# Spacing the indirect DMAs of a routed expert layer by the expert blocks, with TensorE's attention slots put in another order

## The reference

```python
x = x + tanh(g_xattn) * attention(layernorm(x), ctx, ctx)   # 16 heads of 16, 77 keys per batch, float32
x = x + tanh(g_ffn) * moe(layernorm(x))

def moe(x):                        # 4096 rows, 8 experts, W1 (8, 256, 512), W2 (8, 512, 256)
    probs = softmax(x @ Wg)
    top_w, top_i = top_k(probs, 2); top_w = top_w / (sum(top_w) + 1e-8)
    h = square(relu(x @ W1[e])); y = h @ W2[e]        # for the two chosen experts e of a row
    return sum over the two choices of top_w * y
```

## Time and profile before

| | |
|---|---|
| Median of 3 runs | 614.36 us (608.73 to 615.72) |
| The profiled execution | 608.3 us, its span 606.5 us |
| PE busy | 530.1 us (87% of the span) |
| PEld, DVE, ACT, POOL busy | 482.5, 365.5, 277.5, 240.8 us |
| Mean granted clock of TensorE | 0.953 |
| Chain that ended last, by engine | PE 68%, DVE 14%, issue 8%, "another core or an unknown queue" 5% |
| Gathers (L701) | 64, 0.95 us each on POOL |
| Row stores (L692) | 64, 1.02 us each on POOL |

### The profile page before, as it was taken

How to read it: one execution, slowest core, us unless ns; L and a number is a source line. 1 busy time by engine, 2 the same in 40 slices (tenths; PEclk the granted TensorE clock), 3 DMA queues, 4 the chain that set the end, 5 groups by cost and what they waited for, 6 DMA issues and landing times.

```text
span 606.5 us, 13192 instructions
## 1 busy us (share of the span) xinstructions
PE 530.1 (87%) x4125; PEld 482.5 (80%) x4125; DVE 365.5 (60%) x934; ACT 277.5 (46%) x564; POOL 240.8 (40%) x346
## 2 busy tenths in 40 slices
PE   5789999889999999988988699999939997979780
PEld 3688999879898888977777689999839996969670
DVE  5665576585766777854675854454416774736452
ACT  3455455544555453634543345555425553535330
POOL 5154446756677455637126300000343543040422
PEclk9799999999999998978999989999979998989986
DMA  7102222342433531536326463222334775553423
GB/s 252 37 2 89 88 79 65 120 132 84 136 106 96 175 105 36 166 130 202 112 69 194 135 207 110 81 75 77 103 95 145 225 217 166 154 157 107 138 89 120
DMA packets 63873, 73.93 MB, mean 122 GB/s; under 512 B 8128, under 2 KB 56512, under 8 KB 63808
## 3 DMA queue, kind: packets, MB, share of 16 engines
q1 hardware_dynamic: 56560, 55.45, 29.2%
q0 software_dynamic: 6272, 16.79, 8.7%
q10 hardware_dynamic: 976, 0.84, 0.5%
HBM read 42.78 MB, written 32.37 MB: 124 GB/s over the span
## 4 chain that ended last, share of the span: by engine, by line
PE 68%; DVE 14%; issue 8%; another core or an unknown queue 5%; ACT 2%; POOL 1%; DMA 0%; POOLq 0%; DVEq 0%; ACTq 0%
PE pair L931 38%; PE pair L1116 10%; PE pair L1017 5%; PE pair L968 4%; DVE top L1357 3%; PE pair L1118 2%; PE pair L999 2%; PE pair L1177 1%; PE pair L1058 1%; DVE st L1398 1%; PE pair L1038 1%; DVE hsq L1310 1%; DVE attn L1370 1%; DVE xgTlo L1314 1%
## 5 line engine op out<-in xcount | busy, mean ns | idle before, releaser
L701 POOL DMA_INDIRECT ys<-y_scratch,list_at x64 | 60.8, 950 | 192.5 <-DMA y_scratch<-y_sb 133.7
L931 PE MATMUL pair<-w2hi,hThi 128*128 x284 | 86.9, 306 | 9.5 <-issue 5.2
L1300 DVE TENSOR_TENSOR hTlo<-pair,hThi 128x512 fp32r<-128x512 f32 x71 | 49.0, 691 | 66.7 <-ACT hThi L792 47.4
L1310 DVE TENSOR_TENSOR hsq<-pair,hrelu 128x512 f32<-128x512 f32 x71 | 49.0, 690 | 58.8 <-ACT hrelu L798 45.6
L931 PE MATMUL pair<-w1hi,xgThi 128*128 x142 | 64.1, 451 | 23.3 <-DVE xgTlo L1314 23.3
L931 PE MATMUL pair<-w2lo,hThi 128*128 x284 | 81.8, 288 | 0.0
L931 PE MATMUL pair<-w2hi,hTlo 128*128 x284 | 80.7, 284 | 0.0
L1116 PE MATMUL pair<-long,probT 128*128 128x136 f32 x512 | 77.9, 298 | 1.9 <-issue 1.9
L798 ACT ACTIVATE hrelu<-pair 128x512 f32<-128x512 f32 x71 | 42.5, 598 | 72.8 <-PE pair L931 60.3
L692 POOL DMA_INDIRECT xe_scratch<-stage,list_at x64 | 65.5, 1024 | 25.1 <-issue 12.8
L1116 PEld LDWEIGHTS pair<-long,probT 128*128 128x128 f32 x512 | 68.4, 201 | 3.5 <-issue 2.1
(11 more groups left out here) (180 smaller groups left out, 1278.1 us busy)
## 6 DMA issues: line engine op xcount, KB each, us to landing
xg<-xe_scratch SPq DMA_DIRECT2D x71, 128.0 KB
y_scratch<-y_sb SPq DMA_DIRECT2D x71, 128.0 KB
raw<-in_L_ffn_W SPq DMA_DIRECT2D x16, 512.0 KB
xs<-in_x SPq DMA_DIRECT2D x16, 256.0 KB, 3.8
x_scratch<-xs SPq DMA_DIRECT2D x16, 256.0 KB, 2.2
xn_scratch<-xn SPq DMA_DIRECT2D x16, 256.0 KB
stage<-xn_scratch SPq DMA_DIRECT2D x32, 128.0 KB
x1s<-x_scratch SPq DMA_DIRECT2D x32, 128.0 KB, 3.3
```

Source lines behind the costliest of these rows:

```text
L701: pool.indirect_dma_start(ys[t % YB][:, k, :].bitcast(I32), None, y_dram[:, :], bass.IndirectOffsetOnAxis(ap=list_at[:, k, t:t + 1], axis= ...
L931: mm = pe.matmul(dst, l(k), r(k), start=(k == 0 and i == 0), stop=(k == n - 1 and i == 2))
L1300: dve.tensor_tensor(hTlo[j % 2][:, :, :].rearrange("p c n -> p (c n)"), bank[2 + j % 2][:, :], hThi[j % 2][:, :, :].rearrange("p c n -> p ...
L1310: dve.tensor_tensor(hsq[i % 2][:, :], bank[i % 2][:, :], hrelu[:, :], ALU.mult).then_inc(v_hsq, 1)
```

## The change

Row stores: one a slot up to slot 66, two from there (64 as before). From slot 65 on, the first store of a tile waits for the hThi copy of its slot's block j (`a_hT` at j+1) and the second for the hrelu copy of the same call (`a_relu` at j+3). Gathers: `plan_gathers` gives each of the 64 a half-block of its own, with the same kind of waits; each choice has its own semaphore, and VectorE's sum waits for the two one after the other. The sums stand one block earlier than before (tile 0 in block 36, not 37); tile 31's moves from 77 to 75. The last routing group's first tile gets its own count: one more matmul on TensorE and, on VectorE, `mid`, `open0`, `opened0` ahead of the last list of places, so that tile 30 is gathered once 69 blocks are written, tile 31 once all 71 are. TensorE's slot: the value and bias products come ahead of the scores (from slot 1 on); the long scores come first, the short ones after the maximum product and the weighted values; in slots without a query product the weighted values come ahead of the maximum product. ScalarE and VectorE follow that order. The four tables are converted in slot 0.

```diff
-        EARLY, BIAS, TABLES = SLOTS[0] + 1, 1, 3
+        EARLY, BIAS, TABLES = SLOTS[0] + 1, 1, 0
...
-                take = 1 if s < UNITS - 8 else 2
+                take = 1 if s < UNITS + 3 else 2
...
-            return min(NJ, max(STARTS[1] + E, CHOICES * (t0 + n) + E - 1))
-        def plan_sums():
-            at_tile = {}
+            known = t + 1 if t0 + n == NT else t0 + n
+            return min(NJ, max(STARTS[1] + E, CHOICES * known + E - 1))
+        def plan_gathers():
+            at_half, sum_slot, last = {}, {}, 0
             for t in range(NT):
-                j = max(sum_after(t) + 5, max(at_tile) + 1 if at_tile else 0)
-                at_tile[j] = t
-            return at_tile
-        def y_load_at(t):
-            free = [j + 1 for j in sum_at if sum_at[j] == t - YB]
-            return max([sum_after(t) + 3] + free)
+                free = sum_slot[t - YB] + 1 if t >= YB else 0
+                for k in range(CHOICES):
+                    last = at_half[t, k] = max(last + 1, 2 * (sum_after(t) + 2), 2 * free)
+                sum_slot[t] = max(last // 2 + 2, sum_slot.get(t - 1, 0) + 1)
+            return at_half, {j: t for t, j in sum_slot.items()}
...
-                       [None, None, "place", "count", "placed", "at", "open", "opened"],
+            if r == len(GROUPS) - 1:
+                return [None, None, "place", "mid", "open0", "opened0", "count", "placed", "at", "open1", "opened1"]
+            return [None, None, "place", "count", "placed", "at", "open0"] + ["opened0"] * (r > 0)
...
-            def store_rows(r, t, k):
+            def store_rows(r, t, k, s):
                 i = t % STAGES
+                j = ffn_at(s) if s > FFN + 2 else None
+                if j is not None and k == 0:
+                    pool.wait_ge(a_hT, j + 1)
+                if j is not None and k == 1:
+                    pool.wait_ge(a_relu, j + 3)
                 pool.wait_ge(v_route, routed_at["at", r])
...
-            def gather_y(t):
+            def gather_y(t, k, half):
                 for i in range(FLIGHT):
                     pool.wait_ge(d_y[i], 16 * len(range(i, sum_after(t), FLIGHT)))
                 if t >= YB:
                     pool.wait_ge(v_sum, CHOICES * (t - YB + 1))
-                for k in range(CHOICES):
+                j, late = divmod(half, 2)
+                if j < NJ and not late:
+                    pool.wait_ge(a_hT, j + 1)
+                if j < NJ - 2 and late:
+                    pool.wait_ge(a_relu, j + 3)
...
-            for j in range(max(sum_at) + 1):
-                for t in range(NT):
-                    if y_load_at(t) == j:
-                        gather_y(t)
+            for t in range(NT):
+                for k in range(CHOICES):
+                    gather_y(t, k, gather_at[t, k])
...
-                    act.wait_ge(t_short, v + 1)
+                    act.wait_ge(t_long, v + 1)
                     if v >= 2:
                         act.wait_ge(t_pv, v - 1)
-                    act.activation(probT[v % 2][:, CHUNKS, :], bank[4][:, 0:GT * P], ACT.Exp, scale=DH ** -0.5)
+                    act.activation(probT[v % 2][:, 0:CHUNKS, :].rearrange("p n q -> p (n q)"),
+                                   pair[1][:, :, :].rearrange("p j n -> p (j n)"), ACT.Exp, scale=DH ** -0.5)
                     act.wait_ge(t_score, v + 1)
...
+                u, v = max_unit(s), pv_half(s)
+                if v is not None and q_group(s) is None:
+                    weighted_values(v)
+                if u is not None:
+                    max_product(u)
+                if v is not None and q_group(s) is not None:
+                    weighted_values(v)
+                if nv is not None and s <= 0:
+                    value_product(nv)
+                if vs is not None:
+                    for i, (k, q) in enumerate(passes):
+                        mm = pe.matmul(bank[4][:, 0:GT * P], k[:, MAIN:KW], q, start=(i == 0), stop=(i == 3))
+                    mm.then_inc(t_score, 1)
...
-                dve.wait_ge(d_ys[t % YB], 16 * CHOICES * (t // YB + 1))
                 dve.wait_ge(d_x1s[t % YB], 16 * (t // YB + 1))
                 for k in range(CHOICES):
+                    dve.wait_ge(d_ys[t % YB][k], 16 * (t // YB + 1))
```

147 lines of the change are left out of this document (79 added, 68 removed).

## The result

The changed kernel takes 579.57 us (median of 4, 576.49 to 581.99), the kernel before 611.71 beside it (608.73 to 615.72). The ratio is 0.947, 95% interval 0.942 to 0.952: 32 us faster. The sum had -45.4 for the profiled execution (608.3 to 562.9); that of the changed kernel took 576.49, so 13.6 us of the expected gain are missing.

The account below looks back on a forecast made before the run. TensorE bounds the kernel (PE busy 87%), with 76.4 us of gaps, largely from trains of indirect DMAs. Terms -27.4 - 9 + 1 - 3 - 7 = -45.4 take 608.3 to 562.9; plus 2 gives 565, range 551 to 583.

Parts of the forecast that it names:

- Rival 1: Gathers and row stores: DMA traffic costs, not the train, so the loss is only spread; 599 us, chance 6%.
- The gathers: -27.4 taken: Blocks 34 to 69: spacing gathers by half-blocks removes four trains' 28.57 us, adding 1.2 for pairs; -27.4 us.
- the good stretch of pairs: Blocks 37 to 48, gathers in pairs, one per block: 38.85 us for 38.25, a cost of 0.60 us.
- The row stores: -9 taken: Slots and first blocks: spreading the stores removes most of a 12.7 us loss; -9 us, between 0 and -12.7.
- the one at 316: The burst of eight row stores at 316 to 327 us, PE working 7.23 of 11.10, to spread over four blocks.
- The last tiles: +1 and -3 taken: Added VectorE steps in the routing cost +1 us; two gathers fewer behind the last block save 3 us.
- The slots: -7 taken: TensorE's new slot order: maximum -2, value products -4, tables -1; together -7 us, between -16 and +6.
- the expected wait for the exponentials: TensorE's weighted values wait about 0.5 us for both exponentials in each of 16 slots: 8 us.
- Rival 2: Slots: weighted values wait longer for the short exponential, +9 in place of -2; 579 us, chance 15%.
- Blocks 0 to 12: -1.8 taken: First blocks: -2.8 us of the row stores' gain and +1 for the last tiles' added VectorE steps.
- Rival 3: Gathers landing later than 7.5 us stop VectorE, then TensorE; slower, 629 us at 2 us late, chance 3%.
- The two us added for the level of the other runs: Whole time: the profiled execution lay 6 us below the three runs' median, so 562.9 was raised to 565.

Follow-up runs that it names:

- the plain loads: The kernel before with each gather replaced by a plain load of 128 consecutive rows, same place and queue: 569.6 us, ratio 0.937.
- the pairs: The changed kernel without the gathers' waits on hrelu, so a tile's two gathers go as a pair behind hThi: 577.76 us, ratio 0.949.

## Why the prediction was right, and where it was short

*Direction and mechanism: right.* The gathers in trains cost what was taken from them, the rows 0.36 and 0.68 of the earlier trace rows were rightly read as speaking against traffic, and the gain is some 70% of what was summed (31.8 of 45.4 us). What it is in a train that hangs the others stays open, as the prediction had said. And there was luck in the chip: the one trace from the chip where the kernel before takes 568 us shows no such loss to take away. Rival 1 is refuted by its own test: the plain loads keep the DMA engines at 0.75 in these blocks without a gap of PE. The section "Issuing engines are not separate DMA queues" of "DMA: Bandwidth & Descriptors" in the Trainium skill is about who shares the DMA engines; with them shared that far, PE still had no gap here (10.44 of 10.44 us), so the loss lay elsewhere.

*The gathers: -27.4 taken, -22.6 alone, -22.1 in blocks 34 to 69.* The step that failed is that hThi and hrelu are 1.4 and 2.1 us apart, "more than the 0.95 us that a gather takes on POOL, so no train forms". These distances hold for an undisturbed ScalarE, and up to block 39 the gathers came as foreseen. From block 40 on the copies often stand 0.5 to 0.6 us apart, and both ties are met together. I had read the good stretch of pairs as the nearest row, and it is the nearest in rate, but its pairs followed VectorE's sums. The run with ties to TensorE restores the rate: 69.55 us for 20 blocks, where the prediction's sum implies 70.6. So the ties named were wrong, not the price of a spaced gather.

*The row stores: -9 taken, -8.1 alone (-4.2 to -12).* Right in size as far as can be told. Up to block 0, 6.2 was taken, and 4.3 (beside the kernels of the same group) to 7.9 (beside the trace before) came. But "the one at 316 is spread over four blocks" failed: six of them ran as a train at 304.75, as POOL was late behind norm2's statistics. I had named what waits behind the gathers on GpSimd, and not what the stores themselves wait behind. It cost some 3.5 us, as the variant with the stores tied to TensorE shows.

*The last tiles: +1 and -3 taken.* The +1 came, or a little more: in the kernel with this part alone block 11 takes 1.6 us longer. Of the -3 that kernel has 2.3. In the whole, from the last hThi copy on, it turned into 18.9 for 18.1, by the condition the text had named: if these gathers "stall the last copies, the 3 go back to 0". I had named it and given it no weight in the sum. That mending it gains nothing was beyond the text: behind the last copy the same gathers bind the end.

*The slots: -7 taken.* Measured: 0 (2.3 either way) by the ratio of this part alone, -2.3 up to block 0 beside the kernels of its group, -2.8 there between two traces from different chips, and -4.8 (-0.9 to -8.7) by the ratios with and without it. The term was probably taken too large, though -7 still lies inside the last interval. Its terms fell otherwise than I put them: the wait for the maximum lost 8.2 and not 2, since the expected wait for the exponentials is 0.6 and not 8; in exchange a wait for xs of 3.8 and one of 2.4 before the bias products came, which I hadn't named. The waits together fall by about the 7 us of the sum, the time by less; where the rest stays isn't shown. Rival 2, that the weighted values wait longer for the exponential, did not happen.

*Blocks 0 to 12: -1.8 taken, +2.4 measured.* The +2.4 itself is no more than traces of the same code differ by there (57.19 and 61.53). What can be seen is the stores' train again, and block 11, which took 11.11 us for 7.91. In it four stores, the tables and the added VectorE steps meet; the added steps alone make it 9.52. The rest isn't separated.

*Rival 3,* a late gather that stops VectorE, did not come: of VectorE's waits before its sums for a gather, 8.5 us in five places, all lie behind 558 us, in the end.

*The time:* 579.57 lies inside the range of 551 to 583, in its upper part. The two us added for the level of the other runs had their reason: the profiled execution is again the fastest, 3.1 us below the median. That the trains' cost "is probably what varies between runs, and it goes" isn't borne out: runs of the changed kernel still vary by 5.5 us, those of the variant with all ties on TensorE by 0.9, but those of the pairs, which have trains, by 1.3.

## What to carry to other kernels

Where other engines hang while one queue issues indirect DMAs back to back, space them, and tie the spacing to something that they do not move. Here ties to TensorE's matmul groups kept 1.6 and 1.9 us between starts and lost nothing (69.55 us for 20 blocks); ties to ScalarE's copies bunched (73.9 us). A wait for a count only holds back what is early; what can come late (behind statistics, at the end) needs its place in the queue or a later count, and the gaps it leaves must be looked for in the timeline. Take a baseline on more than one chip before such a cost is given to the program: the kernel before took 568 us on one chip and 601 to 620 on the others.

## What the runs showed of the hardware that was not expected

- Trains of indirect DMAs from GpSimd (0.95 us each, 1.25 from start to start) go with waits of ScalarE of 2 to 7 us that nothing shown ends, with the DMA engines at 0.36 or 0.23 of their time (the halved gathers). Not every train of four does: in the kernel with ties to TensorE four from 544.10 to 547.86 left it no "remote" wait (the next hThi copy came 4.53 us after the one before it, for 3.48). Twelve plain DMAs of the same bytes from the same queue, 0.54 us each, hold nothing at 0.75, on a chip where the kernel before takes 39 us more, 33 of them in the gathers' stretches by the traces.
- The size doesn't matter: with 64 rows in place of 128 an indirect DMA takes 0.90 for 0.95 us, and the train's blocks 24.37 for 22.37 to 24.58.
- On one of the chips the train of 12, reading consecutive rows, and the unchanged trains of row stores hold nothing: PE is busy 14.85 of 14.85 us beside the 12, and the kernel before is 7% faster than on the others. Why wasn't found.
